# Middle stage: the second gates loaded over the rotation's tables, and their multiply moved from GpSimd to VectorE

## The reference, cut to what matters

```python
h = _layernorm(x) * (1 + ca) + sa
x = x + ga * _L0_attn_ref(h, ...)       # 32 query heads, rotary embedding by cos/sin tables
h = _layernorm(x) * (1 + cb) + sb
x = x + gb * _L0_ffn_ref(h, weight, scale_param)   # the gate gb is the one that moves
# the feed-forward part: h @ sign(weight).T, times a scale per output column, nan_to_num
h = _layernorm(x) * (1 + ca) + sa       # layer 1: attention over the heads of one row
x = x + ga * _L1_attn_ref(h, ...)
```

## Time and profile before

| What | us |
|---|---|
| median of 3 runs | 2146.93 (2145.73 to 2150.25) |
| the profiled execution, its own time | 2148.18 |
| its span from the first to the last instruction | 2146.3 |
| stage `mid`, half 0 | from 846.6 on, the next stage's first work at 976.3 |
| stage `mid`, half 1 | from 1898.0 on, the next stage's first work at 2027.0 |

### The profile page before, as it was taken

How to read it: one execution, slowest core, us unless ns; L and a number is a source line. 1 busy time by engine, 2 the same in 40 slices (tenths; PEclk the granted TensorE clock), 3 DMA queues, 4 the chain that set the end, 5 groups by cost and what they waited for, 6 DMA issues and landing times. The chain is left out here.

```text
span 2146.3 us, 33364 instructions
## 1 busy us (share of the span) xinstructions
PE 1968.8 (92%) x11441; PEld 1600.4 (75%) x11441; DVE 1481.6 (69%) x3676; ACT 1066.6 (50%) x2418; POOL 1051.6 (49%) x809
## 2 busy tenths in 40 slices
PE   4899999999999997797848999999999999987797
PEld 3788888888888875475527888888888888845664
DVE  4667676776767665956776776676776667789286
ACT  3555555555555552434235555555555555543332
POOL 3556564645656432544046555655555565527231
PEclk8999999999999998898979999999999999998899
DMA  5010101011010234236321001010110100131561
GB/s 173 20 30 20 31 20 30 21 30 50 21 30 20 78 102 149 71 96 131 85 87 51 27 8 46 21 30 21 30 47 8 45 20 1 37 136 40 122 121 40
DMA packets 132006, 115.30 MB, mean 54 GB/s; under 512 B 43200, under 2 KB 93440, under 8 KB 131840
## 3 DMA queue, kind: packets, MB, share of 16 engines
q1 hardware_dynamic: 124784, 105.51, 17.1%
q10 hardware_dynamic: 7056, 7.68, 1.2%
HBM read 92.15 MB, written 16.81 MB: 51 GB/s over the span
## 5 line engine op out<-in xcount | busy, mean ns | idle before, releaser
L896 ACT ACTIVATE gqa_prob<-gqa_prob,gqa_nmax 128x256 f32<-128x256 f32 (+3 forms) x512 | 284.1, 556 | 152.3 <-DVE gqa_nmax L1026 144.0
L906 ACT CAST gqa_pth<-gqa_pT 128x384 fp32r<-128x384 f32 (+1 forms) x384 | 185.7, 519 | 182.1 <-PE gqa_pT L729 179.5
L1026 DVE CUSTOM_DVE_ANT_0 gqa_prob<-gqa_pS,consts 128x256 f32<-128x256 f32 (+3 forms) x512 | 222.8, 486 | 59.6 <-PE gqa_pS L691 57.5
L1198 POOL TENSOR_TENSOR x<-x,consts 128x512 f32<-128x512 f32 x80 | 107.1, 1338 | 302.2 <-ACT x L880 302.2
L1198 POOL TENSOR_TENSOR y<-y,consts 128x512 f32<-128x512 f32 x80 | 107.3, 1341 | 286.8 <-ACT y L880 286.7
L1034 DVE TENSOR_TENSOR gqa_ptl<-gqa_pT,gqa_pth 128x384 fp32r<-128x384 f32 (+1 forms) x384 | 216.8, 592 | 18.3 <-ACT gqa_pth L906 18.0
L729 PE MATMUL gqa_pT<-consts,gqa_prob 128*128 128x128 f32 x1280 | 184.8, 276 | 19.2 <-DVE gqa_ptl L1034 13.3
L669 PE MATMUL gqa_pj<-first_hh,wqh 128*128 128x512 f32 x496 | 196.3, 396 | 0.0
L669 PE MATMUL gqa_pj<-first_hh,wql 128*128 128x512 f32 x496 | 194.8, 393 | 0.0
L669 PE MATMUL gqa_pj<-first_hl,wqh 128*128 128x512 f32 x496 | 194.1, 391 | 0.0
L1050 DVE TENSOR_SCALAR gqa_prob<-gqa_prob,gqa_rden 128x128 f32<-128x128 f32 (+3 forms) x512 | 188.8, 431 | 4.6
(11 more groups left out here) (371 smaller groups left out, 5464.0 us busy)
## 6 DMA issues: line engine op xcount, KB each, us to landing
shared<-in_wo SPq DMA_DIRECT2D x16, 1024.0 KB, 5.3
shared<-in_wq SPq DMA_DIRECT2D x14, 1024.0 KB, 5.6
shared<-in_wmod SPq DMA_DIRECT2D x10, 1024.0 KB, 5.2
raw_kv<-in_wkv SPq DMA_DIRECT2D x14, 512.0 KB, 6.9
vp<-mid_hf SPq DMA_DIRECT2D x64, 64.0 KB, 1.8
kp<-mid_hf SPq DMA_DIRECT2D x16, 256.0 KB, 2.3
qp<-mid_hf SPq DMA_DIRECT2D x16, 256.0 KB, 2.7
tail_bd<-vp SPq DMA_DIRECT2D x64, 64.0 KB, 3.2
```

Source lines behind the costliest of these rows:

```text
L896: ins = nc.scalar.activation(p, p, ACT.Exp, scale=-1.0, bias=nmax[r][:, i:i + 1], accum_out=den[r][:, i:i + 1])
L906: nc.scalar.copy(pth[:, n % 2, c:c + w], pT[k % 2][:, 0:w]).then_inc(pt_hi, 1)
L1026: nc.vector.tensor_tensor_reduce(prob[r][:, P_OFF[i]:P_OFF[i] + w], pS[s][:, c:c + w], held.mask[:, T - w:T], -1.0, LARGEST, ALU.add, ALU.min,
L1198: nc.gpsimd.tensor_tensor(rot[r % 2][:], rot[r % 2][:], held.sinT, ALU.mult).then_inc(sined, 1)
```

## The change

The second gates get a place of their own: the columns of `consts` that hold the rotation's tables, which no stage reads between one half's `gqa` and the next. SP loads them near the head of the stage `mid`, behind the column scale `rs` and ahead of the projection weights, without a wait. DVE multiplies each examined tile with them at the head of `second_residual`, and each tile's sum and statistics now follow its own `examine`, where they had stood up to two tiles later. POOL's list after its first three multiplies is now a wait for `ready` at 2 and then low parts alone. In the stage `tail` of half 0, SP loads the rotation's tables again, ahead of the rows for half 1.

```diff
@@ stage_middle, SP
                 signs.load(sp)
+                for b in range(HB):
+                    sp.dma_start(gate2[:, b, :], a["gates"][1, half * HB + b:half * HB + b + 1, :].to_broadcast([P, D])).then_inc(gate_in, 16)
                 qkv.load(sp)
                 for loaded in later:
                     loaded.load(sp)
-                sp.wait_ge(own_gated, 1)
-                sp.wait_ge(gated, TT - 1)
-                load_gates(sp, held, a, 1, half, gate_in)
                 sp.wait_ge(put, NT)
@@ stage_middle, POOL
-                for j in range(TT):
-                    apply_gate(j)
+                pool.wait_ge(ready, 2)
                 for n in range(KT):
                     qkv.lo_of(pool, n)
-                apply_gate(TT)
-                low(2, (0, 1))
-                apply_gate(TT + 1)
-                low(2, (2, 3))
-                apply_gate(TT + 2)
-                qkv.lo_of(pool, KT)
-                qkv.lo_of(pool, KT + 1)
-                apply_gate(TT + 3)
-                for n in range(KT + 2, 3 * KT):
+                low(2, range(KT))
+                for n in range(KT, 3 * KT):
                     qkv.lo_of(pool, n)
@@ stage_middle, DVE
                 def second_residual(j):
+                    dve.wait_ge(put, j + 1)
+                    if j == 0:
+                        dve.wait_ge(gate_in, 16 * HB)
+                    nc.vector.tensor_tensor(y[:, j, :], y[:, j, :], gate2[:, j // TT, :], ALU.mult).then_inc(z_gated, 1)
                     dve.wait_ge(z_gated, j + 1)
                     summed(1, j)
...
                         examine(j)
-                        if j % TT >= 2:
-                            second_residual(j - 2)
-                    second_residual(b * TT + 2)
-                    second_residual(b * TT + 3)
+                        second_residual(j)
                     normalise(1, b)
@@ stage_heads_and_finish, SP
                 if half + 1 < B // HB:
+                    sp.dma_start(held.consts[:, 0:2 * T], a["tables"][:, 0:2 * T]).then_inc(tables_in, 16)
                     sp.wait_ge(s_full, CU * (UNITS1 - NK // 2))
...
                 if half + 1 < B // HB:
+                    sp.wait_ge(tables_in, 16)
                     sp.wait_ge(next_in, 16 * HB)
@@ build
+        held.gate2 = held.consts[:, 0:2 * T].rearrange("p (b d) -> p b d", b=HB)
```

More of the change, by code:

```diff
@@ L201, in landed, with load_gates @@
         sp.wait_ge(self.came, 16 * 2 * HB)
-def load_gates(eng, held, a, which, half, sem):
+def load_gates(eng, gate, a, which, half, sem):
     for b in range(HB):
-        eng.dma_start(held.gate[:, b, :], a["gates"][which, half * HB + b:half * HB + b + 1, :].to_broadcast([P, D])).then_inc(sem, 16)
+        eng.dma_start(gate[:, b, :], a["gates"][which, half * HB + b:half * HB + b + 1, :].to_broadcast([P, D])).then_inc(sem, 16)
     eng.wait_ge(sem, 16 * HB)
@@ L609, in _ @@
                     sp.wait_ge(v_turned, UNITS)
-                    load_gates(sp, held, a, 0, half, gate_in)
+                    load_gates(sp, held.gate, a, 0, half, gate_in)
                 for j, (l, c) in enumerate(later):
@@ L1250, in stage_middle @@
     with Stage(nc, f"mid{half}") as st:
-        x, y, hh, hl, gate = held.x, held.y, held.hh, held.hl, held.gate
+        x, y, hh, hl, gate, gate2 = held.x, held.y, held.hh, held.hl, held.gate, held.gate2
         sgn, rs = signs.sgn, signs.rs
@@ L1334, in low @@
                         nc.gpsimd.tensor_tensor(hl[:, k, t], hf[0][:, k], hh[:, k, t].bitcast(F32), ALU.subtract).then_inc(h_lo, 1)
[L1336 to L1339, removed]
                 for j in range(TT, NT):
@@ L1623, in stage_heads_and_finish @@
         v_in = [st.sem(f"v_in{u}") for u in range(UNITS1)]
-        next_in = st.sem("next_in")
+        next_in, tables_in = st.sem("next_in"), st.sem("tables_in")
         k_zeroed = st.sem("k_zeroed")
```

## The result

The changed kernel took 2158.09 us (median of 6 runs, 2153.46 to 2161.14), the kernel before 2147.63 beside it (6 runs): a ratio of 1.0047, 95% interval 1.0034 to 1.006. Slower by 10.5 us, 1.1 us from the forecast 2157. In a second set of 6 runs it took 2156.04 against 2148.0, 1.0033 (1.002 to 1.0046).

What follows compares the result with a forecast made beforehand. In `mid`, DVE set the pace up to `ready`, then PE narrowly; DVE would now be late at `turn(3)`. (1.6 + 2.0) + (2.25 + 2.0) + 2.3 = 10.2 us on 2146.93 gave 2157, range 2151 to 2163.

Steps and rivals of the forecast that it cites:

- T0: Moment of `ready` in `mid`, start of tile 4 on DVE: 25.8 us after tile 0, 2.2 and 2.6 earlier.
- rival 3: Gates land only at 869 and stop DVE's first multiply by some 7.6 us a half: 2172 us, chance 0.03.
- Tiles 4 to 7: DVE in `mid`: POOL's 16 splits cost 13.3 us, first normalised rows at T0 + 39.6, 3.8 and 4.85 later.
- rival 1: Faster: POOL's splits hardly hold DVE (0.42 each), PE leads at `turn(3)`: 2140 us, chance 0.12.
- rival 2: No difference: splits cost 9 us, 0.56 each, `last_xn` at T0 + 35.3: 2146.5 us, chance 0.16.
- PE's wait: In `mid`, PE idles some 6.5 us for DVE's rows; `turn(3)` starts 1.6 and 2.25 us later.
- The two waits for `qkv_wl`: PE's waits for POOL's low parts in `mid`, 1.9 us: they go, but the gain is worth nothing.
- The clock: PE's slower clock behind the idle stretch before `turn(3)` costs 2.0 us a half; bounds 0 and 3.
- SP's queue: In `mid`, 16 stores of values move to about 918, covered; without cover up to 2 us a half.
- The reload: In `tail` of half 0, 512 KB ahead of the rows cost 2.3 us, once; bounds 0.6 and 4.
- The sum: Both halves' `turn(3)` delays and clock terms plus the reload: 10.2 us slower, median 2157.
- wait of 4 to 5 us: Sign of a right forecast: PE waits this long for `shared<-tail_o` in `tail` of half 0.

Runs made afterwards that it cites:

- e1: Changed kernel with POOL's four splits of the q weights moved behind the last normalised rows: 2151.99 us, ratio to the kernel before 1.0022.
- e2: Changed kernel without POOL's wait for `ready`, its 12 weight splits running from the start of `mid`: 2157.15 us, ratio to the kernel before 1.0048.
- e6: Changed kernel without DVE's second-gate multiplies and the two waits for them: 2145.46 us, ratio to the kernel before 0.9997.
- e5: Changed kernel without the reload of the rotation's tables: 2153.18 us, ratio to the kernel before 1.0031.
- e9: Changed kernel with the reload behind the loads of the attention output: 2153.49 us, ratio to the kernel before 1.0036.
- e3: Kernel before plus the reload of the tables alone: 2149.01 us, ratio to the kernel before 1.0007.
- e11: Changed kernel with 12 splits on DVE, a weight's four merged, reload and next half's input behind the attention output's loads: 2141.43 us, ratio to before 0.997.

## Why the prediction was right, point by point

**T0.** 25.8 forecast, 25.79 measured, and half 1 had 25.81. (The multiply's 0.72 is 0.73 by the rows that the forecast names; a tile alone took 5.72 for its 5.71.) Nothing else was late, and the gates came in time: DVE shows no wait for them, which ends rival 3.

**Tiles 4 to 7.** 39.6 forecast, 39.14 + 0.5 measured in half 0. What POOL's 16 splits cost was 13.3 in the forecast; tiles 4 and 5 lost (12.18 + 12.60) - 2 x 5.72 = 13.3, 0.83 a split, and e1 and e2 measure 0.7 to 0.88 by taking splits away and by moving them. That leaves no room for rival 1 (0.42 each) or rival 2 (0.56). The term's form held in detail: seven of a tile's nine instructions stretch, the multiply out of PSUM and the statistics don't. Of the 4.8 us that the forecast added to this stretch (34.8 to 39.6), 3.5 are the four multiplies and 1.3 the denser splits; POOL had 16 instructions there before, too, only with pauses between them. e6 prices the multiplies as forecast.

The Trainium skill (SBUF — State Buffer, section "SBUF: two separate sides") says that GpSimd and a DVE instruction with two SBUF inputs, or in a mode that uses both of DVE's ports, exclude each other for the whole instruction. The trace agrees on the sum and the new multiply, with two SBUF inputs (1.60 to 1.67 in place of 0.69), and on the product out of PSUM, which has one (0.67 as before); `mid_clip` with its one input was held as well, and no run here shows in which mode it ran. By the full hold a split would cost its whole time, about 1.3 (5.21 for four in e1); the 14 held instructions of tiles 4 and 5 lost 0.95 each.

**PE's wait.** `turn(3)`, measured from the stage's first instruction on DVE (846.63 before, 846.78 after; 1898.02 and 1903.58 in half 1), came 1.8 and 2.5 us later (1.6 and 2.25 forecast), behind waits of 7.47 and 6.88 (about 6.5). The two waits for `qkv_wl` went and were worth nothing, as forecast.

**The clock.** 2.0 a half forecast. The stage grew by 4.67 and 4.37 us in all; from `turn(3)` to its end it takes 57.86 and 56.92 us, where the kernel before takes 54.97 and 55.01. These 2.9 and 1.9 are the clock's: PE shows no other wait there, and in e2, where it starts `turn(3)` at once, the stretch has 54.97 and 54.98 again. In the second trace of the changed kernel they are 1.9 and 2.1, with a granted clock of 0.60 and 0.85 in the first two of the windows shown above. The size moves from run to run by about 1 us.

**SP's queue.** The 16 stores of values went out from 918.85 (about 918 forecast), and DVE's turned blocks showed no wait for them.

**The reload.** 2.3 forecast. The sum came out right here partly by luck: between the traces the mid stages took 9.0 (8.7 between the second ones) where the forecast had 7.85, and `tail` 0 took 0.97 (1.53) where it had 2.3, since the kernel before loses 2 us in that place that the changed kernel doesn't. What the reload costs by itself is not settled. It is 2.7 to 4.0 in single traces, without what the projection can add; in the times, the changed kernel's two ratios (1.0047 and 1.0033) and those of e5 and e9 (1.0031 and 1.0036) overlap in their intervals, and e3's interval holds no change at all. That the reload comes on top of PE's wait for the copies behind it was right as a mechanism (e5, e9, e11); its wait of 4 to 5 us stood in e2, e3 and e6, not in the changed kernel.

## What to carry to other kernels

An engine's idle time is a place to put work only if its instructions don't hold the engine that is late: price a moved instruction by what it does to the neighbour, per pair, and not by its own time. Here the same subtraction cost the late engine 0.83 us when POOL did it and 0.6 when DVE did it itself. The multiply cost DVE 0.73 as its own and about as much before, when POOL did it (0.75 an instruction in the prediction's count, an average over gates and splits), so moving it gained DVE nothing. The right swap was the other one. And a load that isn't needed soon belongs behind the loads that an engine waits for, even if it is small: that is how PE's wait went in e9 and e11, though its price in time is not settled here.

## What was not expected of the hardware

POOL and DVE, where they block each other, go about one for one (14 held instructions of DVE beside POOL's 16 in tiles 4 and 5) and still overlap: an instruction of 0.7 us on DVE with one of about 1.3 on POOL takes 1.5 to 1.75 us, not 2.0. The short instructions (0.42 alone, 1.50 here) lose more than the long ones (0.69 alone, 1.60 here).

The transposes behind a wait of 1.62 us on PE still ran in 1.94, and behind 2.43 and 2.53 us in 3.47 and 3.49. In `tail` of half 0, the same code waited 2.77 and 2.48 us for its copies in the two traces of the kernel before and 0.60 in the one of the changed kernel without the reload; no experiment here explains it. Nor does the length of a wait alone tell what follows: the projection took 10.57 behind 2.77 us and 13.61 behind 2.48.
